# Counts beside the marks, a smaller memset, and a last row block taken half by half, in a three-layer graph network on one core

## What is computed

```python
deg = clip(sum(adj, axis=1) + 1, 1)
z   = concat([x, (adj @ x + x) / deg]) @ W0 + b
out = relu(z);  out = out / max(norm(out), 1e-12)
x1  = layernorm(x + out)
y = x1
for k in range(2):
    y = tanh(concat([adj @ y, y]) @ W1[k])
result = layernorm(x1 + y)
```

## Time and profile before

| | |
|---|---|
| median of 3 runs | 1273.65 us (1273.53 to 1277.28) |
| the profiled execution | 1273.58 us |
| its span | 1271.7 us |
| TensorE (PE) busy | 1195.5 us, 94% |
| VectorE (DVE) busy | 988.7 us, 78% |
| ScalarE (ACT) busy | 899.5 us, 71% |
| GpSimd (POOL) busy | 96.8 us, 8% |
| read from HBM | 270.88 MB |

### The profile page before, as it was taken

The page is one execution under the profiler, slowest core; times in us unless marked ns, Lnnn a source line. Parts: engine busy times, 40 slices in busy tenths (PEclk is TensorE's granted clock), DMA queues, the critical chain, the costliest instruction groups (busy, mean ns, idle before and its releaser), DMA issues.

```text
span 1271.7 us, 25078 instructions
## 1 busy us (share of the span) xinstructions
PE 1195.5 (94%) x9510; PEld 819.7 (64%) x9510; DVE 988.7 (78%) x2641; ACT 899.5 (71%) x1310; POOL 96.8 (8%) x81
## 2 busy tenths in 40 slices
PE   3889989989999999999999999899999999999996
PEld 2445645645655655655655556778888888887775
DVE  7888898798898797798698687876655454778895
ACT  5778878778778678678668565675555555888783
POOL 3000020020020020010020011100000000010211
PEclk9899999999999999999999999899999999999998
DMA  9999999999999999899899880000000000000000
GB/s 322 381 385 370 372 377 364 366 381 356 364 374 375 343 350 379 319 355 361 309 359 346 322 323 4 1 1 1 1 1 1 1 1 1 1 9 9 18 17 19
DMA packets 88042, 274.64 MB, mean 216 GB/s; under 512 B 22384, under 2 KB 22384, under 8 KB 87920
## 3 DMA queue, kind: packets, MB, share of 16 engines
q1 hardware_dynamic: 86880, 272.73, 58.3%
q10 hardware_dynamic: 1040, 0.26, 0.1%
HBM read 270.88 MB, written 2.10 MB: 215 GB/s over the span
## 4 chain that ended last, share of the span: by engine, by line
PE 68%; DVE 15%; DMA 7%; POOL 4%; ACT 3%; issue 3%; DVEq 0%; POOLq 0%; ACTq 0%
PE acc L657 27%; PE acc L826 25%; DMA raw<-in_adj 7%; PE ps_pack L648 6%; DVE marks L905 6%; PE ps_epi L686 3%; ACT raw L467 3%; DVE planes L923 2%; PE ps_pack L788 2%; PE ps_pack L786 2%; POOL root L589 2%; DVE packed L910 1%; POOL root L582 1%; PE ps_epi L766 1%; PE ps_epi L801 1%
## 5 line engine op out<-in xcount | busy, mean ns | idle before, releaser
L467 ACT ACTIVATE raw<-raw 128x1024 f32<-128x1024 uint32 x512 | 535.8, 1048 | 193.2 <-DVE marks L905 192.0
L657 PE MATMUL acc<-planes,feats 128*128 128x512 fp8e4 x2512 | 569.1, 382 | 7.8 <-issue 7.8
L657 PEld LDWEIGHTS acc<-planes,feats 128*128 128x128 bf16 x2512 | 238.7, 98 | 279.6 <-issue 16.6
L905 DVE TENSOR_SCALAR marks<-raw 128x2048 uint8<-128x2048 f32 x256 | 314.4, 1241 | 26.2 <-DMA raw<-in_adj 25.8
L503 ACT ACTIVATE wide<-twos 128x2048 fp32r<-128x2048 fp8e4 x114 | 215.8, 1917 | 111.1 <-PE acc L826 100.8
L1129 DVE TENSOR_SCALAR wide<-twos 128x2048 fp32r<-128x2048 uint8 x114 | 139.4, 1223 | 74.8 <-PE acc L826 74.1
L648 PE MATMUL ps_pack<-pow,marks 128*128 128x64 bf16 x4096 | 141.8, 194 | 44.8 <-DVE marks L905 44.7
L648 PEld LDWEIGHTS ps_pack<-pow,marks 128*128 128x128 fp8e4 x4096 | 135.8, 98 | 67.7 <-issue 58.8
L923 DVE TENSOR_SCALAR planes<-packed 128x128 uint32<-128x128 uint32 x1024 | 150.9, 220 | 23.3 <-DVE packed L910 22.9
L826 PE MATMUL acc<-wide,x_high 128*128 128x512 f32 x512 | 126.7, 394 | 2.5 <-DVE wide L1129 2.2
L910 DVE TENSOR_SCALAR_CACHE_REDUCE packed<-ps_pack 128x512 uint8<-128x512 f32 x128 | 88.0, 687 | 36.8 <-PE ps_pack L648 36.6
(11 more groups left out here) (151 smaller groups left out, 960.5 us busy)
## 6 DMA issues: line engine op xcount, KB each, us to landing
raw<-in_adj SPq DMA_DIRECT2D x256, 1024.0 KB, 6.2
zpart<-in_x SPq DMA_DIRECT2D x7, 256.0 KB, 7.7
out<-result SPq DMA_DIRECT2D x7, 256.0 KB, 2.6
zpart<-in_x ACTq DMA_DIRECT2D x1, 256.0 KB, 9.2
out<-result SPq DMA_DIRECT2D x2, 128.0 KB, 2.0
w_own<-in_L_gnn_W SPq DMA_DIRECT2D x8, 16.0 KB, 6.5
w_a<-in_L_gnn_W SPq DMA_DIRECT2D x4, 16.0 KB, 6.6
w_y<-in_L_gnn_W SPq DMA_DIRECT2D x2, 16.0 KB, 6.7
```

Of the source, the lines that this page charges most:

```text
L467: ins = act.activation(words, words.bitcast(U32), ACT.Sign, accum_out=nonzero[:, tile:tile + 1, I])
L657: mm = pe.matmul(acc[g][:, h, :], feats[g][:, I * TB + a, :], planes[:, h, a, :], start=(start or g in opens) and a == 0, stop=a == TB - 1 ...
L905: dve.tensor_scalar(out_ap.bitcast(U8), raw[:, u, :], 1.0, 64.0, ALU.is_equal, ALU.mult).then_inc(marked, 1)
```

## The change

Three things are changed. (1) ACT's count of a piece waits for the piece's landing, not for its mark, and writes the Sign into the room of `twos` as bytes. SP waits for both the count and the mark before it refills a slot. `kept_y` moves to `agg[0]`, and the save of the sums waits for its use. (2) The memset of `feats` group 2 moves from POOL to VectorE and covers the 8 tiles of one block. (3) Row 3's units are ordered by half; their bits are spread per unit; half 0 of the last row is weighed, passed through tanh and finished from inside the loop over units, and half 1 behind it.

```diff
--- before.py
+++ after.py
@@ -78,13 +78,18 @@
         for col in range(NB - 1, row, -1):
             units += halves(row, col, 1, 1)
     for row in LAST_ROWS:
-        for col in list(range(1, row + 1)) + [0]:
-            units += halves(row, col, 0, 1)
+        cols = list(range(1, row + 1)) + [0]
+        if row == LAST_ROWS[-1]:
+            units += [(row, col, h, 0, 1) for h in range(2) for col in cols]
+        else:
+            for col in cols:
+                units += halves(row, col, 0, 1)
     return units
 
 
 UNITS = unit_order()
 NU = len(UNITS)
+LAST_UNITS = NU - 2 * (LAST_ROWS[-1] + 1)
 THIRD = min(u for u, unit in enumerate(UNITS) if unit[4] and unit[1] <= unit[0])
 AHEAD = 3
 
@@ -136,6 +141,7 @@
     return CLOSED[(kind, ROWS[k]), 1]
 
 
+LAST_HALF = CLOSED[("low", LAST_ROWS[-1]), 0]
 OWN_AFTER = [6, 9, 15] + [min(last_of(k) + 2, NU - 1) for k in range(3, 2 * NB)]
 UPPER_AFTER = [None, 16, 21] + [last_of(k) + 2 for k in range(3, NB)]
 TURN_AFTER = [3, 7, 11, 17] + [last_of(k) + (6 if k < NB else 3) for k in range(3, 2 * NB - 1)]
@@ -211,9 +217,9 @@
         src = sb("src", [P, TB * D], F32)
         z = sb("z", [P, TB * D], F32)
         twos = sb("twos", [P, 2, TB * 4, NW], U8)
-        kept_y = twos[:, 0].rearrange("p a n -> p (a n)").bitcast(F32)
-
-        sq = agg[0][:, 0:TB * D]
+        signs = twos[:, :, :, :].rearrange("p h a n -> p h (a n)")
+
+        sq = kept_y = agg[0][:, 0:TB * D]
         rest = agg[1][:, 0:TB * D]
         nonzero = sb("nonzero", [P, NB * TB, NB], F32)
 
@@ -373,7 +379,7 @@
         C1 = 6
 
         BITS = 1 + 2 * QH
-        CONSTS = 4
+        CONSTS = 3
         WEIGHTS = 16 * 18
 
 
@@ -415,6 +421,7 @@
                     for u in range(4):
                         if J + k > 0:
                             sp.wait_ge(counted, 4 * (J * NB + k) + (u - 3))
+                            sp.wait_ge(marked, 4 * (J * NB + k) + (u - 3))
                         sp.dma_start(raw[:, u, :].rearrange("p (q c) -> p q c", q=2),
                                      adj_t[J, I, :, 2 * u:2 * u + 2, :]).then_inc(raw_landed[u], 16)
                         if J == 0 and u == 1 and k < NB - 1:
@@ -460,11 +467,14 @@
             def count_step(J, s):
                 k, h = divmod(s, 2)
                 for u in (2 * h, 2 * h + 1):
-                    act.wait_ge(marked, J * 4 * NB + (4 * k + u + 1))
+                    act.wait_ge(raw_landed[u], J * (16 * NB) + 16 * (k + 1))
+                    slot = 4 * (J * NB + k) + u
+                    if slot > 1:
+                        act.wait_ge(counted, slot - 1)
                     for q in range(2):
                         words = raw[:, u, q * BLK:(q + 1) * BLK]
                         tile, I = J * TB + (2 * u + q), ORDERS[J][k]
-                        ins = act.activation(words, words.bitcast(U32), ACT.Sign,
+                        ins = act.activation(signs[:, u % 2, q * BLK:(q + 1) * BLK], words.bitcast(U32), ACT.Sign,
                                              accum_out=nonzero[:, tile:tile + 1, I])
                     ins.then_inc(counted, 1)
 
@@ -473,6 +483,8 @@
                 act.wait_ge(product_done, J * STEPS + STEPS - 1 + h)
                 if h == 0 and J > 0:
                     act.wait_ge(x1_ready, J)
+                    if J > 4:
+                        act.wait_ge(y_pair_ready, J - 4)
                     act.wait_ge(epi_drained, USES_1 * J)
                 for g in range(GROUPS):
                     ins = act.activation(agg[g][:, h * HALF:(h + 1) * HALF], acc[g][:, h, :], ACT.Copy, scale=0.5)
@@ -535,6 +547,11 @@
                 act.wait_ge(own_read, k + 1)
                 act.activation(ap, ap, ACT.Tanh).then_inc(tanh_done, 1)
 
+            def last_tanh(half):
+                act.wait_ge(own_read, 2 * NB + half)
+                ap = result[:, (2 * NB - 1) % 2, 4 * half * D:4 * (half + 1) * D]
+                act.activation(ap, ap, ACT.Tanh).then_inc(tanh_done, 1)
+
             save_acc(NB - 1, 0)
             for u in range(NU + AHEAD + 8):
                 if u < NU:
@@ -544,16 +561,14 @@
                 for k in range(2 * NB):
                     if TURN_AFTER[k] + 3 == u:
                         save_turned(k)
+                if u == LAST_HALF + 4:
+                    last_tanh(0)
                 for key in closed_at(u - 2):
                     save_sum(key)
                 for k in range(2 * NB):
                     if ADD_AFTER[k] + 1 == u and k < 2 * NB - 1:
                         take_tanh(k)
-            last = result[:, (2 * NB - 1) % 2]
-            for half in range(2):
-                act.wait_ge(own_read, 2 * NB + half)
-                ap = last[:, 4 * half * D:4 * (half + 1) * D]
-                act.activation(ap, ap, ACT.Tanh).then_inc(tanh_done, 1)
+            last_tanh(1)
 
             with act.If(unless_binary(act) > 0):
                 for L in (1, 2):
@@ -588,10 +603,9 @@
                 pool.wait_ge(pool_step, n)
                 pool.tensor_tensor(root[:, cols], stat[:, cols], minus_half[:, cols], ALU.pow).then_inc(root_ready, 1)
 
-            pool.memset(feats[YHI // P][:, :, :], 0.0).then_inc(consts, 1)
             pool.memset(minus_half[:, :], -0.5).then_inc(consts, 1)
             pool.memset(ident[:, :], 0.0).then_inc(consts, 1)
-            pool.wait_ge(consts, 3)
+            pool.wait_ge(consts, 2)
             pool.affine_select(out=ident[:, :], in_=ident[:, :], compare_op=ALU.not_equal, fill=1.0,
                                base=0, pattern=[[-1, P]], channel_multiplier=1).then_inc(consts, 1)
 
@@ -714,7 +728,7 @@
                         pe.wait_ge(x_ready, k + 1)
                     groups = range(2)
                     if J == 0 and k == opening:
-                        pe.wait_ge(consts, CONSTS)
+                        pe.wait_ge(lo_zeroed, 2)
                         groups = range(3)
                     elif I < J:
                         pe.wait_ge(x1_ready, I + 1)
@@ -768,7 +782,7 @@
                                            start=n == 0, stop=n == 1, skip_group_check=True)
                 mm.then_inc(turned, 1)
 
-            def weigh_own(k):
+            def weigh_own(k, part=range(2)):
 
                 kind, w_of, w, sums = ("one", w_y_self, w_y_pair, agg[1]) if k < NB else ("low", w_x2_self, w_x2_pair, agg[k % 2])
                 pe.wait_ge(turn_saved, k + 1)
@@ -776,7 +790,7 @@
                     pe.wait_ge(checked, 4)
                 else:
                     pe.wait_ge(own_read, k)
-                for half in range(2):
+                for half in part:
                     pe.wait_ge(sums_saved, SAVED[(kind, ROWS[k]), half])
                     for t in range(4):
                         tile = 4 * half + t
@@ -843,7 +857,9 @@
                     check_sums()
                 for k in range(2 * NB):
                     if OWN_AFTER[k] == u:
-                        weigh_own(k)
+                        weigh_own(k, range(2) if k < 2 * NB - 1 else [1])
+                    if k == 2 * NB - 1 and LAST_HALF + 2 == u:
+                        weigh_own(k, [0])
                     if k < NB and UPPER_AFTER[k] == u:
                         weigh_upper(k)
                     if TURN_AFTER[k] == u:
@@ -1063,6 +1079,7 @@
                             keep_y(J - 1)
 
             dve.memset(feats[YLO // P][:, :, YLO % P:YLO % P + D], 0.0).then_inc(lo_zeroed, 1)
+            dve.memset(feats[YHI // P][:, 0:TB, :], 0.0).then_inc(lo_zeroed, 1)
             for pair in range(2):
                 mark(0, 0, pair)
             split_x(0)
@@ -1085,17 +1102,21 @@
             def two_bits(u):
 
                 row, col, h = UNITS[u][:3]
-                if u >= THIRD:
+                if THIRD <= u and row != LAST_ROWS[-1] or THIRD <= u < LAST_UNITS and row == LAST_ROWS[-1]:
                     if h == 0:
                         two_bits_pair(u)
                     return
-                if u >= 2:
+                if u >= LAST_UNITS:
+                    if u % 2 == 0:
+                        dve.wait_ge(low_ready, u - 2)
+                        dve.wait_ge(high_ready, u - 2)
+                elif u >= 2:
                     dve.wait_ge(low_ready, u - 1)
                     dve.wait_ge(high_ready, u - 1)
                 elif u == 0:
                     dve.wait_ge(y_pair_ready, 3)
                 words = words_of(row, col, h)
-                room = twos[:, u % 2].rearrange("p (a g) n -> p a (g n)", a=TB).bitcast(U32)
+                room = twos_of(u).rearrange("p (a g) n -> p a (g n)", a=TB).bitcast(U32)
                 for g in range(4):
                     ins = dve.tensor_scalar(room[:, :, g * NW // 4:(g + 1) * NW // 4], words, 6 - 2 * g, 0xC0C0C0C0,
                                             ALU.logical_shift_left, ALU.bitwise_and)
@@ -1249,6 +1270,7 @@
                     ins.then_inc(normed, 1)
 
             LAST = 2 * NB - 1
+            FIRST_LAST = LAST_HALF + 4
 
```

(11 more changed lines are left out.)

## The result

The changed kernel took 1269.05 us in the median of 18 runs (1266.05 to 1270.75), the kernel before 1273.76 us (1269.69 to 1277.91, 18 runs). The ratio is 0.9962, with a 95% interval of 0.9952 to 0.9971: faster by 4.7 us, just over the 3.8 us that the prediction took as the least that can be told from none. The forecast was 1266.5 us, 7.2 us less. The changed kernel's profiled execution has a span of 1267.3 us, where before had 1271.7.

What follows compares the result with a forecast made beforehand. The prediction took the supply of pieces to bound the first 400 us and TensorE the rest. Supply -7.5, opening -2.0 and last row block +2.3 sum to -7.2 us, giving 1266.5 us; range 1260.5 to 1274.5.

Steps and rivals of the forecast that it cites:

- Opening: Start of the kernel: without POOL's memset the first mark is short and the first pack earlier; 2.0 us gained.
- Supply: Matrix reading: slots freed earlier raise the DMA rate; 7.5 us gained, 5.0 of it in 100 to 300 us.
- The rule against it: Matrix reading: HBM limit of about 358 GB/s for one core, by which earlier free slots would bring nothing.
- Rival 1: Matrix reading: DMA engines are at their limit, freed slots only queue longer; 1274.0 us, chance 0.24.
- The last row block: End of the kernel: VectorE's queue order delays row 4's reduce, the x1 sum and half 1; 2.3 us lost.
- The lower bound: Last row block: if VectorE never waited for half 0's chain, a gain of 0.7 us.
- Rival 3: Block changes: ACT stands at the save of sums, pieces lie uncounted, SP starves; slower, 1280.5 us, chance 0.08.
- Rival 2: End and supply both gain: row 4's chain runs ahead of half 0, supply gives everything; 1261 us, chance 0.10.

Runs made afterwards that it cites:

- counts_only: Kernel before with only ACT's counts run from the landing, old memset and last row kept; 1266.34 us, ratio 0.994.
- last_only: Kernel before with only the last row block taken half by half, stage one unchanged; 1277.17 us, ratio 1.0015.
- memset_counts: Changed kernel without the new order of the last row block; 1266.91 us, ratio 0.9939; run again 1266.25 us, ratio 0.9932.
- light_counts: memset_counts with six of eight TensorE products and most VectorE planes left out in stage one; 1179.15 us, one execution.
- late_half: Changed kernel with half 0's steps one unit later and half 1's steps 0 to 2 before half 0's last multiply; 1266.2 us, ratio 0.9925; again 0.9938.
- light_before: Kernel before with the smaller VectorE memset, six of eight TensorE products and most VectorE planes left out in stage one; 1214.54 us, one execution.

## Why the prediction was right, point by point

**Opening.** The cause (POOL's memset) and the time of the first pack held: 10.79 us, forecast 10.9. The term of 2.0 us in the whole is not a term of its own. The gap in the DMA engines is filled once, by either edit, which the sum did not see: alone the memset measures 3 us, on top of the counts nothing that the runs can tell (ratios 0.9940 without and 0.9939 with it, intervals of 0.2% on either side). The 2.4 us of lead at the 500th matmul come near the 2.0 by luck, since the counts alone bring 2.2. The exclusive lock on a port pair that the Trainium skill states in "SBUF — State Buffer", section SBUF: two separate sides, agrees with the traces: with the memset gone the mark is back at 1.23 us, and in counts_only, where it stays, the first mark takes 6.55 us.

**Supply.** The mechanism held: a slot freed earlier, three pieces in flight for more of the time, a higher rate. Two of the signs that I had named came out at their very edge: packs wait 20.0 us in 20 to 400 (less than 20), and the rates of 100 to 200 and 200 to 300, 386 and 364, have a mean of 375 (375 or more). Two sizes were off. I took the rate of 40 to 100 us, 382 GB/s, as the most the engines would give; they gave 386 in 100 to 200 in this kernel and 406 with nothing else in the way. And I put 5.0 us on 100 to 300 us because TensorE idled there and the DMA share was 0.99. The gain is 3 us in 100 to 200 and none in 200 to 300: the idle time there is VectorE's epilogue ahead of marks, shown for three of its five gaps. From 300 to 400 us 1.1 us came (forecast 1.5), later nothing (1.0). The row that tells them apart is the wait of marks for raw pieces in that stretch alone, 1.1 us; I had read that wait only over 20 to 400 us as one sum. Opening and supply together were forecast at 9.5 us. The traces show 6.6 at the end of stage one, or 8.9 if last_only's trace stands for the kernel before; the medians of memset_counts and its repeat show 8.4 and 7.7. So this term was too large, by 0.6 to 2.9 us according to which of these is taken. The 2.5 us by which the whole missed the forecast lie here, since the end came out within 0.3 us.

**The rule against it.** "DMA: Bandwidth & Descriptors", section Specifications, of the Trainium skill gives about 358 GB/s as HBM's limit for one core. No run here agrees: 370 GB/s before, 386 after, 407 in light_counts. The measurement decides. Rival 1, which stood on the limit, is out by light_counts.

**The last row block.** Forecast 2.3 us, measured 2.0 in the traces, by the steps named: row 4's reduce behind half 0's step 0, the x1 sum late, half 1 behind all of half 0. Row 4's reduce starts 1.5 us later against row 2's (24.71 us behind it, 23.26 before), forecast 1.95; from there to the end it takes 0.6 us more, forecast 0.3. The lower bound, a gain of 0.7 us if half 1 never waited, is what late_half shows, 0.6.

**Rival 3.** ACT does stand at the save of the sums now, 26.7 us in 12 waits between 20 and 764 us, where before no such wait of it shows in that stretch. No loss followed: from the 500th matmul on the lead over before grows or stays level in stage one. SP waits 488 us for marks and 119 for counts, which fits; whether the stand costs a little was not tried.

**Rival 2** gave 1261 us and needed both the end and the supply to gain; the changed kernel does neither to that extent.

## What to carry to other kernels

A busy share near 1.0 of the DMA engines does not say that they are at their limit; the test is a light kernel in which nothing else binds, with more or less in flight. Before a stall is put down to supply, read the waits of that stretch alone, both links of them: who waited for the mark, and whether the mark waited for its data. When work is moved ahead on an engine with one queue, look at everything it is put in front of: half 0 came earlier by one unit and delayed the other row, the sum on GpSimd and half 1.

## What the runs showed that I had not expected

The busy share of the DMA engines was 1.02 at 378 GB/s (light_before, 100 to 200 us) and 1.02 at 406 GB/s (light_counts).

TensorE's granted clock fell to 1.2 GHz, half, in single stretches that come in some executions and not in others. From 835 to 855 us it was 1.00 of full speed in the profile of counts_only and 0.91 in that of memset_counts, first and second row here:

```profile
835.00:855.00 20.00, 18.01 (x95) 15.09 (x93) 16.50 (x43) 12.83 (x10) 0.00 (x0) 1.00 0.01 1
...
835.00:855.00 20.00, 18.01 (x89) 15.05 (x88) 15.03 (x36) 12.85 (x10) 0.00 (x0) 0.91 0.00 1
```

In memset_counts the clock fell at 844 us, behind 2.0 us in which TensorE stood for VectorE; counts_only has the same wait and no fall. TensorE was busy alike in both, and counts_only came out of this part of stage two 2.4 us further ahead of memset_counts than it went in (7000th and 7500th matmul). That is more than the whole loss at the end, so a single profile of either kernel does not rank them.
